# First neighbour aggregation between masked sums and attention heads, input stage at the step's end, three rotating x buffers: a four-layer graph network on one Trainium2 core

## The chip, the cores and the metric

One core of one Trainium2 chip runs the whole program. The metric is the device time of one execution in microseconds (us). The core has five engines that run their own instruction streams and meet only at semaphores: TensorE (PE in the profile; PEld is its weight load), VectorE (DVE), ScalarE (ACT), GpSimd (POOL) and SyncE (SP), the last of which here only issues DMAs.

## What is computed

Eight graphs of N = 1024 nodes with D = 128 features and a 0/1 adjacency matrix of 1024 x 1024 each. Every layer adds its result to its input and normalises the rows:

```python
x = _layernorm(x + _L0_gnn_ref(x, adj, Wq, bq, Wk, Wv, bv))   # masked softmax attention, 1 head
x = _layernorm(x + _L1_gnn_ref(x, adj, W, b))                 # mean over neighbours, linear, leaky ReLU
x = _layernorm(x + _L2_gnn_ref(x, adj, W, a))                 # 4 additive (GAT) heads of 32 features
x = _layernorm(x + _L3_gnn_ref(x, adj, B))                    # normalised adjacency (+ identity), linear
```

In the third layer `e = s_i + s_j`, with a leaky ReLU of slope 0.2, a softmax over the neighbours `i` of each `j`, and the weighted sum of `Wh`. Since exp(leaky(s_i + s_j)) is one product of exponentials where s_i + s_j is positive and another where it is negative, the kernel computes, for each head, sums over the neighbours above the step (matrices `c`, one per head, built from `steps` and `adj`) and sums over all neighbours (`mask` sums), and combines them.

## The kernel before

The rows of a graph lie in T = 8 tiles of 128 on the partitions. The work is pipelined over nine steps: "first" (graph 0 alone), seven "full" steps 1 to 7, and "last". Full step g does layers 0 and 1 of graph g, and layers 2 and 3 of graph g - 1 (called `o` in the code); "last" does layers 2 and 3 of graph 7. The order on every engine is written out by hand; engines are in order, so a wait holds everything behind it on its engine.

TensorE writes into four PSUM buffers of 128 x 1024 float32: three of a `ring`, claimed in turn by the groups of a fixed sequence (`claim` waits until the group three places earlier has been read), and `Z` for what is accumulated over a long time. In a full step TensorE does, in this order:

- **opening**: `xT` (transpose of the new x0), `q`, `v`; `s` 0 to 4 (bfloat16 scores, from which VectorE takes row maxima); between them, for the older graph, `x2T`, `wh` twice and `sj`, the inputs of its heads. At L1138 are `s`, at L1152 and L1165 `wh` and `sj`.
- **softmax**: eight transposed score groups `st` (L1198 adds the mask, L1200 the float32 scores), with `s` 5 to 7 between them, and one group later the `context` (L1222), which multiplies the exponentials that ScalarE made of the group. Two small transposes (`turn_largest` L1178, `spread_largest` L1183) are put between them.
- **heads**: `mask` 0 and 1 (L1235), then `c` 0 to 3 (L1254), one per head.
- **aggregations**: `agg1` (L1271, layer 1 of graph g: 32 matmuls), `out1` (L1287, times W1), `agg3` (L1271, layer 3 of the older graph) with the second half of `out1` inside, and `out3` (L1287) in two halves.

VectorE, for each row tile of the new graph, takes the row maximum of scores and mask (L755), rounds it (L742) and subtracts it from the mask (L747): together `guards`. A transposed score group needs the four mask tiles of its half. VectorE also builds `c` by a minimum of `steps` and `adj` (`mins`, L810), 32 tiles in a full step; evaluates each head (`combine`, L893 to L909); does layer 1's end (`layer1_out`, L927 to L932) and layer 3's (`layer3_out`, L940); the statistics of each norm (L839), its application (L846), and the splits of x into two float32r parts (`split_x1`, `split_x3`: L853, L855, L869).

ScalarE reads the ring (L579, L624), makes `maskb` for the coming graph (L591), the exponentials (`exp_tile`, L661), the `steps` tiles (L654; the list PACE says how many behind each exponential; four buffers, so tile n waits for the minimum of tile n - 4), and widens adjacency tiles from float16 to float32r for the aggregations (L612). These wide tiles have eight buffers: four of `wide_low`, and four of `wide_high`, which lie over `maskb`.

GpSimd computes each norm's rstd (L468, L471), the degrees (L455 to L461), the products of `wh` and `ex` (L497), two of the four subtractions that split them into three bfloat16 parts (L506 twice per piece), adds the identity to the transposed adjacency of the older graph (L526), applies the third norm (L480, L483), and issues the loads of `adj`. SyncE's queue transposes adjacency tiles by DMA: `adjT` for the new graph, and for the older one into `cmat[:, 1]`, which is possible only when head 1 has been computed (`turn_older`: `full["c"]`, 4).

x lives in four buffers: x0 (input), x1, x2 and x3 (after the first, second and third layer). In "last" the row of head 0 is made on TensorE (L1159), not fetched from DRAM.

## Time and profile before

| | |
|---|---|
| time, median of 3 runs | 977.44 us (975.45 to 979.87) |
| the profiled execution | 977.33 us, its span 975.5 us |
| mean granted TensorE clock | 0.957 |
| PE busy | 848.5 us, 87% of the span |
| DVE busy | 731.0 us, 75% |
| ACT busy | 587.1 us, 60% |
| POOL busy | 326.3 us, 33% |
| TensorE in step 5 (528.5 to 642.6 us) | busy 103.76 us of 114.10 |

The profile divides the span by instructions. A number in brackets at the end of a line of its timeline is the idle time of that engine just before, with what ended it. Several instructions of the same kind in a row are one line of the timeline, with their count; the time on it reaches from the first one's start to the last one's end, and includes waits of less than a fraction of a microsecond. Ends of matmuls are modelled, and 0.15 to 0.2 us of each lie beside the next one.

### The profile page before, as it was taken

The numbers are of one execution on the slowest core, as the hardware profiler recorded it, in microseconds if no ns is written. First come the engines' busy times: TensorE is split into PE (matmuls) and PEld (weight loads), VectorE is DVE, ScalarE is ACT, GpSimd is POOL, SyncE is SP. The second block draws the span as 40 slices with busy tenths as digits, with TensorE's granted clock in tenths as the row PEclk, the third lists the DMA queues.
The fourth block names the chain that finished last, engine by engine and source line by source line (L and its number), as shares of the span: only waits on it lengthen the run. The fifth ranks groups of instructions, "written<-read, shape, count | busy, mean of one in ns | idle before, by whom it ended". The sixth has DMA issues, their size and how long they took to land.

```text
span 975.5 us, 25298 instructions
## 1 busy us (share of the span) xinstructions
PE 848.5 (87%) x10856; PEld 683.6 (70%) x10856; DVE 731.0 (75%) x1635; ACT 587.1 (60%) x668; POOL 326.3 (33%) x335
## 2 busy tenths in 40 slices
PE   4988999798998989889998989989899899974874
PEld 2664699556985679746896569856697468962873
DVE  3438777788768787689777887687877798765965
ACT  1564675667665766656846666657665667545513
POOL 2022511633034520626007240355207161064404
PEclk8998999999999999999999999999999999996897
DMA  9823116911178123760268211781237601700260
GB/s 184 123 65 70 41 46 89 164 54 44 50 105 153 45 87 53 121 134 2 87 90 151 66 44 46 97 164 46 76 59 130 111 20 67 89 2 23 67 89 22
DMA packets 166463, 77.39 MB, mean 79 GB/s; under 512 B 136624, under 2 KB 154160, under 8 KB 166352
## 3 DMA queue, kind: packets, MB, share of 16 engines
q1 hardware_dynamic: 156864, 58.48, 31.5%
q0 software_dynamic: 8448, 16.78, 9.7%
q8 instruction: 85, 1.39, 0.6%
q10 hardware_dynamic: 1040, 0.52, 0.2%
q14 instruction: 26, 0.21, 0.1%
HBM read 54.66 MB, written 4.33 MB: 60 GB/s over the span
## 4 chain that ended last, share of the span: by engine, by line
PE 36%; issue 25%; DVE 22%; POOL 7%; ACT 7%; DVEq 0%; POOLq 0%; ACTq 0%
PE ring L1200 7%; PE Z L1222 7%; PE ring L1254 5%; PE Z L1271 4%; DVE x L846 4%; DVE cmat L810 4%; DVE ring L755 3%; PE ring L1235 2%; ACT steps L654 2%; POOL rstd L471 2%; ACT maskb L591 2%; PE ring L1198 2%; DVE meanvar L839 2%; PE ring L1165 1%; DVE x L830 1%
## 5 line engine op out<-in xcount | busy, mean ns | idle before, releaser
L654 ACT ACTIVATE steps<-sjrow,steepsi 128x1024 bf16<-128x1024 f32 x248 | 267.5, 1139 | 123.3 <-DVE cmat L810 94.9
L810 DVE TENSOR_TENSOR cmat<-steps,adj 128x1024 f16<-128x1024 bf16 x180 | 153.6, 896 | 24.6 <-ACT steps L654 22.6
L1254 PE MATMUL ring<-vparts,cmat 128*128 128x66 bf16 x4416 | 146.2, 195 | 16.9 <-DVE cmat L810 12.1
L1222 PEld LDWEIGHTS Z<-vv,probs 128*128 128x128 f32 x1024 | 122.6, 191 | 52.6 <-ACT probs L661 37.3
L1254 PEld LDWEIGHTS ring<-vparts,cmat 128*128 128x128 f16 x4416 | 143.5, 98 | 18.4 <-issue 7.4
L1222 PE MATMUL Z<-vv,probs 128*128 128x129 f32 x1024 | 126.5, 277 | 25.4 <-ACT probs L661 25.4
L1200 PE MATMUL ring<-qT,xT 128*128 128x512 f32 x256 | 139.4, 627 | 0.0
L526 POOL TENSOR_TENSOR cmat<-cmat,ident 128x1024 f16<-128x1024 f16 x8 | 17.1, 2144 | 254.1 <-DMA cmat<-adj 254.1
L755 DVE CUSTOM_DVE_ANT_0 ring<-ring,maskb 128x1024 f32<-128x1024 f32 x64 | 78.3, 1227 | 29.0 <-PE ring L1138 16.3
L661 ACT ACTIVATE probs<-ring 128x1024 f32<-128x1024 f32 x64 | 65.0, 1015 | 52.1 <-PE ring L1200 52.1
L1235 PE MATMUL ring<-vparts,adj 128*128 128x132 bf16 x1536 | 94.0, 222 | 0.0
L1235 PEld LDWEIGHTS ring<-vparts,adj 128*128 128x128 f16 x1536 | 93.3, 96 | 0.1
L1271 PE MATMUL Z<-wide_low,parts 128*128 128x512 f32 x256 | 68.7, 416 | 22.1 <-DVE parts L855 18.6
L846 DVE TENSOR_SCALAR x<-x,meanvar,rstd 128x128 f32<-128x128 f32 x192 | 73.7, 450 | 4.4 <-POOL rstd L471 4.4
L468 POOL TENSOR_SCALAR vareps<-meanvar 128x4 f32<-128x4 f32 x64 | 13.4, 210 | 186.5 <-DVE meanvar L839 185.5
L1271 PEld LDWEIGHTS Z<-wide_low,parts 128*128 128x128 f32 x256 | 48.0, 197 | 36.2 <-DVE parts L855 21.3
L471 POOL TENSOR_TENSOR rstd<-vareps,powers 128x4 f32<-128x4 f32 x64 | 71.1, 1111 | 5.4
L1198 PEld LDWEIGHTS ring<-ident,maskb 128*128 128x128 f16 x512 | 39.1, 99 | 43.8 <-issue 41.2
L1271 PE MATMUL Z<-wide_high,parts 128*128 128x512 f32 x256 | 65.6, 398 | 0.6 <-ACT wide_high L612 0.6
L612 ACT ACTIVATE wide_high<-adjT 128x1024 fp32r<-128x1024 f16 x32 | 31.2, 1048 | 45.5 <-PE ring L1254 45.5
L591 ACT ACTIVATE maskb<-adj 128x1024 f16<-128x1024 f16 x56 | 58.2, 1042 | 0.0
L1271 PEld LDWEIGHTS Z<-wide_high,parts 128*128 128x128 f32 x256 | 46.4, 188 | 10.8 <-ACT wide_high L612 2.4
(126 smaller groups left out, 1376.3 us busy)
## 6 DMA issues: line engine op xcount, KB each, us to landing
adj<-in_adj_dram POOLq DMA_DIRECT2D x16, 1024.0 KB, 13.0
sjrow<-sj_rows SPq DMA_DIRECT2D x31, 512.0 KB, 4.1
out_dram<-x SPq DMA_DIRECT2D x16, 256.0 KB, 2.4
x<-in_x_dram SPq DMA_DIRECT2D x7, 512.0 KB, 4.3
adjT<-adj SPq DMA_TRANSPOSE x64, 3.5
cmat<-adj SPq DMA_TRANSPOSE x64, 4.5
...
```

Of the source, the lines that this page charges most:

```text
L471: pool.tensor_tensor(rstd[:, layer, ts], vareps[:, layer, ts], powers[:, 0:4, 0], ALU.pow)\
L591: act.activation(maskb[:, t, :], adjs[g.parity][:, t, :], ACT.Copy, bias=-NEG, scale=NEG, accum_out=rowacc[g.parity][:, t:t + 1]).then_inc ...
L654: act.activation(steps[:, n % STEPS, :], sjrow[:, h % 2, :], ACT.Relu, bias=steepsi[:, t, h:h + 1], scale=STEEP).then_inc(step_made, 1)
L661: act.activation(probs[:, n % 2, :, :], slot(kind, "st", n)[:, :, :], ACT.Exp).then_inc(read["st"], 1)
L755: dve.tensor_tensor_reduce(out=s, in0=s, in1=maskb[:, t, :], scale=1.0, scalar=LOWEST, op0=ALU.add, op1=ALU.max, accum_out=smax[:, t:t + 1 ...
L810: dve.tensor_tensor(c_of[:, t, :], steps[:, n % STEPS, :], adjs[o.parity][:, t, :], ALU.min)\
L846: ins = dve.tensor_scalar(xn[:, t, :], xn[:, t, :], meanvar[:, layer, t, 1:2], rstd[:, layer, t:t + 1], ALU.subtract, ALU.mult)
L1200: last = pe.matmul(s[:, j, :], xT[:, kt * P:(kt + 1) * P], qT[:, c * 512:(c + 1) * 512], start=False, stop=True, skip_group_check=True)
L1222: last = pe.matmul(zq[:, q, 0:D + 1], probs[:, n % 2, j, q * P:(q + 1) * P], vv[:, kt, :], start=kt == 0 and q % 2 == 0, stop=kt == T - 1, ...
L1235: last = pe.matmul(s[:, j, 0:H * HW], adjs[o.parity][:, t, jt * P:(jt + 1) * P], vparts[:, t, :, part, HW:VW], start=t == 0 and part == 0, ...
L1254: last = pe.matmul(s[:, jt, 0:VW], c_of[:, t, jt * P:(jt + 1) * P], vparts[:, t, h, part, :], start=t == 0 and part == 0, stop=t == T - 1 ...
L1271: last = pe.matmul(Z[:, c, :], parts[:, part, t, :], wide(t)[:, c * 512:(c + 1) * 512], start=t == 0 and part == 0, stop=t == T - 1 and pa ...
```

## The change

The order on TensorE in a full step becomes: `s` 1 to 4, the softmax, `mask` 0 and 1, `agg1`, `c` 0, `out1` twice, `c` 1 to 3, then for graph g `x2T`, `wh`, `wh`, `sj` and mixed with them for graph g + 1 `xT`, `q`, `v`; then `agg3`, `out3` with `s` 0 of graph g + 1 between its halves. One list SEQ over all steps gives each group its place in the ring. The wide tiles are reduced from eight to four buffers (the second four are widened only when TensorE has used the first four), and `adjT` takes both the transposed adjacency of the new graph and, when that has been widened, of the older one. Three buffers rotate for x, each worked on in place through the four layers. VectorE and ScalarE get the same reordering. The subtraction of the values' high part moves from GpSimd to VectorE. PACE becomes two tiles behind every exponential but the first. "last" fetches all four rows from DRAM.

```diff
+    def groups_of(n):
+        def of(graph, *names):
+            return [(name, graph, k) for name, k in names] if 0 <= graph < NB else []
+        seq = []
+        if n == 0:
+            seq += of(0, ("xT", 0), ("q", 0), ("v", 0))
+        if n < 2:
+            seq += of(n, ("s", 0))
+        seq += of(n, *[("s", t) for t in range(1, 5)])
+        for t in range(T):
+            seq += of(n, ("st", t))
+            if t < 3:
+                seq += of(n, ("s", 5 + t))
+        masks, c = [("mask", 0), ("mask", 1)], [("c", h) for h in range(H)]
+        if n < NB:
+            seq += of(n - 1, *masks, c[0])
+        else:
+            seq += of(n - 1, c[0], *masks)
+        seq += of(n, ("out1", 0), ("out1", 1))
+        seq += of(n - 1, *c[1:])
+        if n < NB:
+            seq += of(n, ("x2T", 0)) + of(n + 1, ("xT", 0)) + of(n, ("wh", 0), ("wh", 1)) + of(n + 1, ("q", 0)) \
+                + of(n, ("sj", 0)) + of(n + 1, ("v", 0))
+        seq += of(n - 1, ("out3", 0))
+        if n > 0:
+            seq += of(n + 1, ("s", 0))
+        return seq + of(n - 1, ("out3", 1))
+    SEQ = [group for n in range(NB + 1) for group in groups_of(n)]
+    PLACE = {group: n for n, group in enumerate(SEQ)}
+    assert len(PLACE) == len(SEQ)
...
-    PACE = [0, 2, 2, 3, 3, 2, 2, 3]
+    PACE = [0, 2, 2, 2, 2, 2, 2, 2]
...
-        wide_low = sb("wide_low", [P, T // 2, N], F32R)
+        wide = sb("wide", [P, T // 2, N], F32R)
...
-        wide_high = sharing("wide_high", [P, T // 2, N], F32R)
         cmat = sb("cmat", [P, 2, T, N], F16)
-        adjT_of_older = cmat[:, 1, :, :]
...
-        x1 = sb("x1", [P, T, D], F32)
-        x2 = sb("x2", [P, T, D], F32)
-        x3 = sb("x3", [P, T, D], F32)
+        xs = [sb(f"x_{n}", [P, T, D], F32) for n in range(3)]
+        def x_of(g):
+            return xs[g.base % 3]
...
-        def wide(t):
-            return wide_low[:, t, :] if t < T // 2 else wide_high[:, t - T // 2, :]
-        def uses_until(agg, g, t):
+        def wide_used_by(agg, g, t):
             n = max(0, 2 * g.base - 1) if agg == "agg1" else min(2 * g.base + 2, 2 * NB - 1)
-            return (T - 1) * (n - 1) + t + 1
+            return (T - 1) * n + t - 3 if t >= T // 2 else (T - 1) * (n - 1) + t + 5
...
-                if g.base > 0:
-                    sp.wait_ge(widened["agg1"], g.count(T))
+                if g.base == 1:
+                    sp.wait_ge(widened["agg1"], T)
+                elif g.base > 1:
+                    sp.wait_ge(widened["agg3"], g.before(2).count(T, T))
...
+            def turn_older(kind, o):
+                if kind == "last":
+                    sp.wait_ge(widened["agg3"], o.count(T))
+                else:
+                    sp.wait_ge(widened["agg1"], o.count(T, 2 * T))
...
+                if kind != "last":
+                    if g.base < NB - 1:
+                        sp.wait_ge(y_made[0], g.count(2, 2))
+                        sp.dma_start(x0[:, :, :], x_v[number(Graph(g.base + 1))]).then_inc(x_in, 16)
+                    if kind == "full":
+                        turn_older(kind, o)
+                    spread_sj(g)
+                    for h in (0, 1):
+                        fetch_sj(kind, g, h)
...
-                    if 1 + SPLIT_BY_DVE[kind] <= n < pieces + 1:
-                        take_off(kind, o, n - 1, 0, None, high_made, rest_made)
                     if n >= 2 + SPLIT_BY_DVE[kind]:
-                        take_off(kind, o, n - 2, 1, 2, middle_made, low_made)
+                        low_part(kind, o, n - 2)
...
                 if kind != "last":
                     rstd_of(0, g)
+                    degree_of(g)
+                    for k in range(2):
+                        rstd_of(1, g, [k])
                 if kind != "first":
                     add_diagonal(o)
-                    rstd_of(2, o)
                     if o.base < NB - 2:
                         pool.wait_ge(full["mask"], o.count(2, 2))
                         pool.wait_ge(c_made, o.count(H * T, H * T))
                         load_adj(Graph(o.base + 2))
-                if kind != "last":
-                    degree_of(g)
-                if kind != "first":
+                    rstd_of(2, o)
...
-                    act.activation(wide(t), src, ACT.Copy).then_inc(widened[agg], 1)
+                    if t >= T // 2 or (t < T // 2 - 1 and (agg == "agg3" or g.base > 0)):
+                        act.wait_ge(wide_used, wide_used_by(agg, g, t))
+                    act.activation(wide[:, t % (T // 2), :], adjT[:, t, :], ACT.Copy).then_inc(widened[agg], 1)
...
-                    widen(kind, g, "agg1", range(T))
+                            made = steps_until(made + PACE[n])
+                    widen(g, "agg1", range(0, 4))
+                    if kind == "first":
+                        make_maskb(Graph(1), range(4, T))
+                    else:
+                        made = steps_until(20)
+                    widen(g, "agg1", range(4, T))
                     take_sums("agg1", g, agg1T)
...
+                if kind != "first":
+                    made = steps_until(len(STEP_TILES[kind]))
+                    widen(o, "agg3", range(0, 4))
+                if kind != "last":
+                    following = Graph(g.base + 1)
+                    for name, graph, k in (("x2T", g, 0), ("xT", following, 0), ("wh", g, 0), ("wh", g, 1),
+                                           ("q", following, 0), ("sj", g, 0), ("v", following, 0)):
+                        if graph.base < NB:
+                            take_group(kind, graph if name != "sj" else g, name, k)
+                if kind != "first":
+                    widen(o, "agg3", range(4, T))
+                    take_sums("agg3", o, agg3T)
...
+                if part == 0:
+                    v = VALS[kind][:, :, hs, :]
+                    dve.wait_ge(high_made, o.count(NP, n + 1 - SPLIT_BY_DVE[kind]))
+                    dve.tensor_tensor(v, v, vparts[:, :, hs, 0, :], ALU.subtract).then_inc(rest_made, 1)
...
+                    mins(kind, o, 1, range(0, 4))
+                norm_apply(0, g, x_of(g), 0)
                 split_x1(g, 0)
...
                 if kind == "full":
+                    mins(kind, o, 1, range(4, T))
                     sums_of_masks(kind, o, 0)
-                    mins(kind, o, 2)
-                    sums_of_masks(kind, o, 1)
-                norm_apply(0, g, x1, 1)
+                norm_apply(0, g, x_of(g), 1)
                 split_x1(g, 1)
                 if kind == "full":
+                    mins(kind, o, 2, range(0, 4))
+                    sums_of_masks(kind, o, 1)
+                    mins(kind, o, 2, range(4, T))
                     combine(kind, o, 0)
-                    mins(kind, o, 3)
-                    last_heads(kind, o)
                 for k in range(2):
                     layer1_out(kind, g, k)
-                    norm_stats(1, g, x2, k)
-                final = g.base == NB - 1
-                if kind == "full" and not final:
...
+                if kind == "full":
+                    mins(kind, o, 3, range(0, 4))
+                    combine(kind, o, 1)
+                    mins(kind, o, 3, range(4, T))
+                norm_apply(1, g, x_of(g), 0)
+                norm_apply(1, g, x_of(g), 1)
+                if kind == "full":
+                    combine(kind, o, 2)
+                    end_of_heads(kind, o)
+                    split_x3(o, 0)
+                    split_x3(o, 1)
+                largest_si(g)
+                if g.base < NB - 1:
+                    cast_x(Graph(g.base + 1))
+                    cast_q(Graph(g.base + 1))
+                if kind == "full":
                     layer3_out(kind, o, 0)
...
-                early = [(c, t) for c in range(2) for t in range(T // 2)]
+            def aggregate(of, agg, parts, second_half):
+                early = [(c, t) for t in range(T // 2) for c in range(2)]
                 late = [(c, t) for c in range(2) for t in range(T // 2, T)]
...
                     for n in range(T):
                         scores(kind, g, n)
                         if kind == "full" and n == 0:
-                            turn_largest(kind, g.before())
-                        if between_scores[n]:
-                            group(kind, g, *between_scores[n])
-                        if kind == "full" and n == 0:
-                            spread_largest(kind, g.before())
+                            turn_largest(kind, o)
+                        if n < 3:
+                            guard_scores(kind, g, 5 + n)
+                        if kind == "full" and n == 1:
+                            spread_largest(kind, o)
                         if n >= 1:
                             context(kind, g, n - 1)
```

Three places of the order. The first is TensorE's heads and aggregations in the full steps 2 to 6 (`parts1` marks agg1, `parts3` agg3, `w1_s` out1, `b3_s` out3; `vparts,adj0` are the mask sums, the others with `vparts` the heads 0 to 3). Before:

```order
L1235 MATMUL ring0<-vparts,adj0 128x132 x96
L1254 MATMUL ring1<-vparts,cmat 128x66 x192
L1254 MATMUL ring2<-vparts,cmat 128x66 x192
L1254 MATMUL ring0<-vparts,maskb 128x66 x192
L1254 MATMUL ring1<-vparts,cmat 128x66 x192
L1271 MATMUL Z<-wide_low,parts1 128x512 x16
L1271 MATMUL Z<-wide_high,parts1 128x512 x14
L1287 MATMUL ring2<-w1_s,qT 128x128 x4
```

The same place of the change:

```order
L1249 MATMUL ring0<-vparts,adj0 128x132 x96
L1283 MATMUL Z<-wide,parts1 128x512 x32
L1268 MATMUL ring1<-vparts,cmat 128x66 x192
L1297 MATMUL ring2<-w1_s,qT 128x128 x4
L1297 MATMUL ring0<-w1_s,qT 128x128 x4
L1268 MATMUL ring1<-vparts,cmat 128x66 x192
L1268 MATMUL ring2<-vparts,maskb 128x66 x192
L1268 MATMUL ring0<-vparts,cmat 128x66 x192
```

The aggregation of the new graph and head 0 stand ahead of out1, and the heads 1 to 3 behind it.

The second place is TensorE between out3 and the first transposed scores. Before (`qxb` are the `s` groups, `identf` the two transposes, `wext` wh and sj):

```order
L1287 MATMUL ring2<-b3_s,x2T 128x128 x4
L1109 MATMUL ring0<-identf,x0 128x128 x8
L1122 MATMUL ring1<-xT,wqk 128x512 x2
L1129 MATMUL ring2<-wv_s,xT 128x128 x8
L1138 MATMUL ring0<-qxb 128x512 x2
L1109 MATMUL ring1<-identf,x2 128x128 x8
L1138 MATMUL ring2<-qxb 128x512 x2
L1138 MATMUL ring0<-qxb 128x512 x2
L1152 MATMUL ring1<-wext,x2T 128x136 x4
L1138 MATMUL ring2<-qxb 128x512 x2
L1152 MATMUL ring0<-wext,x2T 128x136 x4
L1165 MATMUL ring1<-x2T,wext 4x512 x2
```

The same place of the change:

```order
L1162 MATMUL ring0<-qxb 128x512 x2
L1297 MATMUL ring1<-b3_s,x2T 128x128 x4
L1162 MATMUL ring2<-qxb 128x512 x2
L1162 MATMUL ring0<-qxb 128x512 x2
L1162 MATMUL ring1<-qxb 128x512 x2
L1162 MATMUL ring2<-qxb 128x512 x2
L1212 MATMUL ring0<-ident16,maskb 128x128 x4
```

Of the projections, transposes and head inputs none stands between the `s` groups any more; they are ahead of agg3.

The third place is VectorE behind head 0 (`small` and `ring` with `probs` begin a `combine`, L945 to L950 are layer1_out, L826 the mins of head 3). The change:

```order
L924 TENSOR_TENSOR x<-small,x 128x8x32
L945 SCALAR_TENSOR_TENSOR rest<-ring,rrow,b_s 128x128 x4
L948 SCALAR_TENSOR_TENSOR rest<-rest 128x512
L950 TENSOR_TENSOR x<-x,rest 128x512
L855 BN_STATS meanvar<-x 128x6 x2
L945 SCALAR_TENSOR_TENSOR rest<-ring,rrow,b_s 128x128 x4
L948 SCALAR_TENSOR_TENSOR rest<-rest 128x512
L950 TENSOR_TENSOR x<-x,rest 128x512
L855 BN_STATS meanvar<-x 128x6 x2
L826 TENSOR_TENSOR cmat<-steps,adj 128x1024 x4
L909 TENSOR_TENSOR small<-probs,ring 128x264
```

Before, the minima of head 3 followed `combine` 0 directly, all eight in a row; now layer1_out with its statistics stands ahead of them, and `combine` 1 between their halves.

## Rows read from the trace of the kernel before

**Rows 1.** Busy time by stretch: step 5 and "last" (us; sum, then engines with counts).
```profile
528.50:642.60 114.10, 103.76 (x1358) 83.84 (x1356) 89.59 (x202) 73.96 (x85) 39.41 (x41) 0.99 0.44 84
874.20:975.50 101.30, 62.08 (x1046) 55.01 (x1044) 71.17 (x151) 39.53 (x40) 36.07 (x36) 0.79 0.25 48
```
**Rows 2.** Waits of TensorE: total us, times, longest.
```profile
PE Z L1222 <- ACT probs L661: 25.4, 19, 1.7
PE Z L1271 <- DVE parts L855: 18.6, 7, 10.7
PE ring L1122 <- ACT xT L579: 16.9, 6, 3.1
```
**Rows 3.** Timeline of TensorE: first transposed scores of steps 1, 2, 5, 7.
```profile
91.78 0.39 PE L1198 MATMUL ring<-ident,maskb 128*128 128x128 f16 x4
...
202.70 0.39 PE L1198 MATMUL ring<-ident,maskb 128*128 128x128 f16 x4
...
545.83 0.39 PE L1198 MATMUL ring<-ident,maskb 128*128 128x128 f16 x4
...
774.53 0.39 PE L1198 MATMUL ring<-ident,maskb 128*128 128x128 f16 x4
```
**Rows 4.** Timeline of TensorE, end of step 4, opening of step 5.
```profile
526.04 0.71 PE L1271 MATMUL Z<-wide_high,parts 128*128 128x512 f32 x2
527.53 1.13 PE L1287 MATMUL ring<-b_s,x2T 128*128 128x128 f32 x8 [0.78 <-ACT x2T L597]
528.50 1.04 PE L1109 MATMUL ring<-identf,x 128*128 128x128 f32 x8
532.59 2.68 PE L1122 MATMUL ring<-xT,wqk 128*128 128x512 f32 x4 [3.05 <-DVE x L940]
```
**Rows 5.** Timeline of VectorE, the same stretch.
```profile
526.98 1.11 DVE L927 SCALAR_TENSOR_TENSOR x<-ring,rrow,b_s 128x128 f32<-128x128 f32 x4
...
530.32 2.14 DVE L940 SCALAR_TENSOR_TENSOR x<-ring,dcol,x 128x128 f32<-128x128 f32 x8
...
538.59 1.23 DVE L755 CUSTOM_DVE_ANT_0 ring<-ring,maskb 128x1024 f32<-128x1024 f32 x1 [1.34 <-PE ring L1138]
...
544.40 0.87 DVE L747 TENSOR_SCALAR maskb<-maskb,guard 128x1024 f16<-128x1024 f16 x2
```
**Rows 6.** Timeline of TensorE: last context, mask sums, a head, end of step 5.
```profile
584.16 2.05 PE L1222 MATMUL Z<-vv,probs 128*128 128x129 f32 x16 [0.93 <-ACT probs L661]
586.05 11.76 PE L1235 MATMUL ring<-vparts,adj 128*128 128x132 bf16 x192
597.65 12.10 PE L1254 MATMUL ring<-vparts,cmat 128*128 128x66 bf16 x384
...
640.11 0.71 PE L1271 MATMUL Z<-wide_high,parts 128*128 128x512 f32 x2
```
**Rows 7.** Timeline of VectorE: minima beside GpSimd, the minimum of tile 7, combine, minima.
```profile
570.27 3.75 DVE L810 TENSOR_TENSOR cmat<-steps,adj 128x1024 f16<-128x1024 bf16 x3
...
578.36 3.09 DVE L810 TENSOR_TENSOR cmat<-steps,adj 128x1024 f16<-128x1024 bf16 x5
...
603.95 0.43 DVE L893 TENSOR_TENSOR small<-probs,ring 128x264 f32<-128x264 f32 x1 [2.73 <-PE ring L1254]
...
606.60 3.69 DVE L810 TENSOR_TENSOR cmat<-steps,adj 128x1024 f16<-128x1024 bf16 x6
```
**Rows 8.** Timeline of GpSimd: a subtraction beside the first of them.
```profile
570.44 2.43 POOL L506 TENSOR_TENSOR vparts<-cmat,vparts 128x1056 bf16<-128x1056 f32 x1 [2.65 <-DVE vparts L793]
```
**Rows 9.** Timeline of "last": VectorE, GpSimd and TensorE ahead of agg3.
```profile
947.01 0.76 DVE L839 BATCH_NORM_STATS2 meanvar<-x 128x6 f32<-128x256 f32 x2
...
948.66 2.11 POOL L526 TENSOR_TENSOR cmat<-cmat,ident 128x1024 f16<-128x1024 f16 x1 [27.82 <-DMA cmat<-adj]
...
955.58 6.14 PE L1271 MATMUL Z<-wide_low,parts 128*128 128x512 f32 x16 [10.67 <-DVE parts L855]
```
**Rows 10.** Timeline of TensorE: end of step 0.
```profile
72.23 1.13 PE L1287 MATMUL ring<-w_s,qT 128*128 128x128 f32 x8 [0.78 <-ACT qT L597]
```

424 lines of the change are left out of this document (183 added, 241 removed).

## The prediction

> **What bounds the kernel now.** I read first the busy time by stretch: in a full step TensorE is busy 103.8 of 114.1 us, in "last" 62.1 of 101.3 [rows 1]. So TensorE bounds the middle, where some 10.3 us of a step are idle, and chains of waits bound both ends. Then the waits of TensorE: three groups make up half of its idle time [rows 2], namely contexts that wait for exponentials (25.4 us), aggregations for the split parts (18.6, of which 10.7 once) and `q` for xT read (16.9, some 3 us a step). Then I took one mark per step, the first transposed score group [rows 3]. Steps 2 to 7 follow each other at (774.53 - 202.70) / 5 = 114.4 us; step 1 takes 110.9; the first mark stands at 91.8; behind the last lie 975.5 - 774.5 = 201.0.
>
> The change does not lessen TensorE's work: the same matmuls, less one group of two in "last". It can only move waits. I therefore lay out a full step in three pieces, from rows of steps 4 and 5, and then both ends. "Mark" is always that first score group.
>
> **Piece 1: from the first half of out3 to the mark.** Before, 526.04 to 545.83: 19.8 us [rows 3, 4], in which stand `xT`, `q`, `v`, `s`, `x2T`, `wh`, `sj`, and the waits 0.78 and 3.05 [rows 4]. Now these projections and head inputs come ahead of agg3: x2T and xT about 1 each (as xT in rows 4), the two wh 2.1, q 2.5, sj 1.8, v 2.75 and 0.4 for x2T to be read: 11.5 us. Between them each reading by ScalarE is covered by the next group, so the 3.05 goes. But behind out3's first half only 3.6 us of work remain: the end of agg3, out3's second half and five `s` groups of 0.44. And VectorE's chain does not get shorter. It has to wait for out3's second half, which is done 2.5 us on; 0.2 for the semaphore and 1.1 for that half of layer3_out (2.14 for both [rows 5]) make 3.8. Then come the guards of tiles 0 to 3, from 538.59 to 545.2, 6.6 us [rows 5], and these have to be complete before the mark. So the mark stands 10.4 us behind, with some 6.7 us idle: guards that were hidden by wh, sj and x2T are bare. Piece 1 becomes 11.5 + 10.4 = 21.9: **+2.1 us**. Here the 3 us won at `q` are given back, and more.
>
> **Piece 2: softmax, from the mark to the mask sums.** Before, 545.83 to 586.05: 40.2 us [rows 3, 6]. The last contexts waited because ScalarE's exponential 6 stood behind a `steps` tile that needed the minimum of tile 7, done about 579.0 [rows 7], and exponential 7 behind two or three more. With PACE at two, only exponential 7 stands behind it. VectorE gets to tile 7 at the same place: behind the mark by 33 to 34 us. Two added subtractions of 1.3 us each (128 x 1056 float32; estimate from 0.69 for 512 columns) fit ahead of context 0, where VectorE waited 2 us; the later place of `spread_largest` costs 1 us more of guards and some 0.7 of the first context, in place of TensorE's wait of 0.8. Step tile 33.8 to 34.9, exponential to 35.9, last context 1.8: mask sums start at 37.9. **-2.3 us**. Bounds: -4.7, if no context waits, and 0, if the subtractions are met by GpSimd's and push tile 7 out.
>
> **Piece 3: mask sums to out3's first half.** Before, 586.05 to 640.11: 54.1 us [rows 6]. Gone is agg3's wait for its parts, 18.6 - 10.7 over six steps: -1.3, since 11.5 us of openings and two splits' margin of about 4 us stand ahead. Four wide tiles in place of eight: a widening and the matmuls on its tile take about 1 us each, with the first four ready: +0.1. agg1 follows the mask sums (11.7 us); its parts need VectorE's context 1, norm and split, about 9.8 us: hidden, the second half by the first. What is new is head 3. Its first accumulation needs all eight minima. From head 0's end VectorE has: 0.3 to start; combine 2.65 (603.95 to 606.60 [rows 7]); layer1_out with statistics, twice 3.34 (526.98 to 530.32 [rows 5]); four minima at 0.62 (3.69 for six [rows 7]); combine 1, 2.65; four minima more, 2.5: together 17.3. TensorE has out1 1.6, two heads of 6.0 (12.1 for two [rows 6]) and 0.65 of head 3 until it asks for tile 7: 14.2. The wait is 3.1, and longer where GpSimd's diagonal addition of 2.1 us [rows 9] falls in: it now comes behind the second rstd of layer 1, so right there. I take +3.5. Piece 3: **+2.3 us**.
>
> What VectorE does next is late with it, but hidden: norm 1 is done 2.2 us behind the last minimum, head 3 takes 5.3, so x2T does not wait; combine 2 and 3, statistics and the splits take until some 7 us behind head 3's end, ahead of agg3, which comes 11.5 behind it. DMA: the transposes of the older adjacency start when agg1 has been widened, 17 us behind the mask sums' start, and take some 16 with their landing; head 3 is over at 48. `adj`, x0 and the rows of s_j are asked for no later than before, relative to their use.
>
> The sum of a step: 2.1 - 2.3 + 2.3 = +2.1, times five: **+10.5**. Step 1 had few waits to lose (no older graph to finish): +1.8 - 0.8 + 2.9 = **+3.9**.
>
> A shared resource decides how far the 3.5 goes up. Three minima took 3.75 beside GpSimd's subtraction of 2.43 us, where three alone take 1.9 [rows 7, 8]: 1.9 us lost for 2.4 of overlap. By that, 2.1 us of diagonal addition cost up to 1.6. The Trainium skill (SBUF — State Buffer, "Who interferes with whom") says that a VectorE instruction with two SBUF inputs and a GpSimd one that reads SBUF exclude each other for a whole instruction. By that, head 3's wait would be anything from 3.1 to 5.2, by who comes first; the sum would lie between -3 and +12 us of mine. These rows agree with it roughly.
>
> **The start.** In step 0 nothing hides the new order. `x2T` needs norm 1 of graph 0, and before, xT, q and v of graph 1 stood in front of it. agg1 with four wide tiles costs 2 more, since four `maskb` tiles stand between them on ScalarE. out1, whose second half began at 72.2 [rows 10], ends at 75; layer1_out twice 3.34 from 74.4, rstd 1.4 and half a norm 1.1 give x2T at 83.8; 12.3 of openings, 0.6 of `s`, 6.6 of guards: mark at 103.4, against 91.8 [rows 3]. **+11.6 us**.
>
> **The end.** Three things. Head inputs of graph 7 and the row of s_j lie before agg3 of graph 6, where VectorE catches up: some 4 to 5 us fewer between the two graphs' heads, after +2 for head 3's wait. The transposes and the diagonal addition, which ended at 950.8 [rows 9], are done long before the heads; then agg3 waits only for statistics (947.77 [rows 9]) and one split of 2.25, so stands at 950.0 and not 955.58: -5.6. Step 7's softmax gives its 2.3. The sum is **-12 us** (189 for 201). Bounds: -6, and -16 if TensorE's clock, which was 0.79 there [rows 1], recovers.
>
> **Sum.** 11.6 + 3.9 + 10.5 - 12 = +14 us on the profiled execution's 977.33, whose span is 975.5, and 0.1 below the median: 991 us.
>
> **The rivals.**
> - *VectorE is in time for head 3* (ends on the other side). If VectorE gained over 3 us between head 0 and tile 7 (or c3 asked later), the wait of 3.5 would be none in seven steps: 991 - 24.5 = 966. For it: all its parts are short instructions that may overlap more than their starts show. Against: the 17.3 are measured start to start; the point of decision is 14.2. Chance 0.12.
> - *The exponentials no longer hold contexts.* Piece 2 at its bound: 2.4 us more in six steps, 991 - 14 = 977: no change. For: PACE gives exponential 6 three microseconds of room. Against: tile 7's place on VectorE. Chance 0.18.
> - *VectorE and GpSimd exclude each other* wherever they were moved together (diagonal addition beside minima, split beside norm 2): 2 us more a step, 1004. Chance 0.15.
>
> **How the numbers follow.** The forecast, slower by 0.7 to 2.2%, has 0.55. The time 991 is that of this case alone. Its own range is 984 to 999; down to 974 for the second rival and half way to the first, up to 1005 for the third. About 0.5% (5 us) is what a measurement here can tell from no change: faster 0.12, the same 0.18, slower 0.70.
>
> **What would show it.** TensorE's waits: `q` for xT gone; about 5 to 7 us a step for VectorE's maxima and guarded `maskb`, at `s` 2, `s` 4 and the mark; a new wait of 3 to 4 for `cmat` in head 3; none for parts in the middle, some 5 us in "last". The first mark near 103, steps of 116.5, 189 behind the last. I would be wrong in the main term if the steps were 114 or shorter: then either `cmat` shows no wait, or the guards end sooner than 10 us behind out3's first half. I would be wrong on piece 2 if contexts still wait 4 us a step.

## The result and the profile after

The changed kernel takes 1004.7 us (median) against 977.1 for the kernel before in the same rounds: ratio 1.0275, 95% interval 1.0244 to 1.0306. Three of its four runs lie between 1003.4 and 1004.8; the fourth took 1238.9 us at a mean granted clock of 0.657 and is left out of the ratio. The change makes the kernel slower, by 27.6 us. The forecast said slower with 0.70 and 991 us, 13.7 too low. 1004.7 lies above the forecast's own range of 984 to 999, and 0.3 below the 1005 that it allowed for its third rival.

The profiled execution took 1003.4 us with a span of 1001.6. The head of its page: busy time by engine, then the granted TensorE clock in 40 slices.

```profile
PE 861.8 (86%) x10852; PEld 690.3 (69%) x10852; DVE 746.3 (75%) x1652; ACT 588.4 (59%) x667; POOL 297.1 (30%) x318
...
PEclk9997899979999999998999999997999999998788
```

TensorE does no more work than before but is busy 13.3 us longer: its mean granted clock is 0.937, before 0.957. The marks (first transposed score group of steps 1, 2, 5 and 7), which answer to [rows 3]:

```profile
102.44 0.59 PE L1212 MATMUL ring<-ident,maskb 128*128 128x128 f16 x4 [3.57 <-DVE maskb L759]
...
218.61 0.59 PE L1212 MATMUL ring<-ident,maskb 128*128 128x128 f16 x4 [3.13 <-DVE maskb L759]
...
572.31 0.44 PE L1212 MATMUL ring<-ident,maskb 128*128 128x128 f16 x4 [3.57 <-DVE maskb L759]
...
807.91 0.53 PE L1212 MATMUL ring<-ident,maskb 128*128 128x128 f16 x4 [3.57 <-DVE maskb L759]
```

None of them waited before; and four small matmuls that took 0.39 us there take up to 0.59.

| part (us of the profiled execution) | before | predicted | after |
|---|---|---|---|
| start to first mark | 91.8 | 103.4 | 102.4 |
| step 1 | 110.9 | 114.8 | 116.2 |
| a step, mean of five | 114.4 | 116.5 | 117.9 |
| behind the last mark | 201.0 | 189 | 193.7 |

Where TensorE waits (total us, times, longest), the rows that answer to [rows 2]:

```profile
PE ring L1268 <- DVE cmat L826: 27.4, 32, 2.4
PE ring L1212 <- DVE maskb L759: 27.3, 8, 3.6
PE ring L1162 <- DVE smax L767: 14.0, 10, 2.0
PE Z L1236 <- ACT probs L664: 9.0, 6, 1.5
```

The waits of `q` for xT are gone, the parts are waited for once (5.1 us, in "last"), contexts wait 9.0 us and not 25.4. In their place come the minima of head 3 (`cmat`), the guarded `maskb` at the mark, and row maxima (`smax`). The stretch around the mark of step 5 on TensorE shows the last two, and what follows them:

```profile
563.40 1.13 PE L1297 MATMUL ring<-b_s,x2T 128*128 128x128 f32 x8 [0.33 <-ACT x2T L611]
564.37 0.59 PE L1162 MATMUL ring<-qxb 128*128 128x512 bf16 x2
566.95 1.79 PE L1162 MATMUL ring<-qxb 128*128 128x512 bf16 x6 [1.99 <-DVE smax L767]
572.31 0.44 PE L1212 MATMUL ring<-ident,maskb 128*128 128x128 f16 x4 [3.57 <-DVE maskb L759]
572.54 2.02 PE L1214 MATMUL ring<-qT,xT 128*128 128x512 f32 x2
574.36 0.63 PE L1212 MATMUL ring<-ident,maskb 128*128 128x128 f16 x4
574.78 1.64 PE L1214 MATMUL ring<-qT,xT 128*128 128x512 f32 x2
```

The matmuls behind out3's first half start at 561.91 and the mark stands 10.4 us on, as worked out. But two score matmuls that take 1.08 us elsewhere take 2.02 and 1.64 here. The busy time by stretch says why (columns as in [rows 1]: stretch, length, PE, PEld, DVE, ACT, POOL, then granted clock):

```profile
562.00:572.31 10.31, 4.28 (x23) 1.85 (x21) 8.87 (x25) 8.90 (x17) 0.00 (x0) 1.00 1.00 172
572.31:577.33 5.02, 5.02 (x20) 2.22 (x21) 1.97 (x5) 0.87 (x1) 0.00 (x0) 0.66 0.02 3
```

TensorE is busy 4.3 of the 10.3 us ahead of the mark, and in the five us behind it the granted clock is 0.66: for part of them it is at 1.2 instead of 2.4 GHz. The loss is a third of 5 us, 1.7 us. This is the milder of two cases that take turns. In steps 2, 4 and 6 the clock is at 1.2 GHz from some 4.5 us ahead of the mark to some 6 us behind it (step 6, around the mark at 689.64); why the two cases take turns was not taken apart:

```profile
685.00:689.64 4.64, 1.41 (x5) 0.17 (x4) 4.64 (x15) 3.89 (x8) 0.00 (x0) 0.51 0.79 149
689.64:694.66 5.02, 5.02 (x14) 1.93 (x14) 1.69 (x4) 0.35 (x1) 0.00 (x0) 0.50 0.02 5
```

From the mark to the mask sums it takes 38.8 us in steps 3, 5 and 7 and 39.8 to 39.9 in steps 2, 4 and 6. A second loss lies in head 3, behind its wait for minima:

```profile
640.00:679.00 39.00, 35.07 (x613) 30.08 (x610) 34.71 (x79) 18.80 (x20) 17.49 (x18) 0.96 0.49 98
```

That is 0.04 of 39 us, 1.6. The kernel before had a loss of this size too, but only one a step: ahead of its mark, where `q` and `v` run behind the wait of `q`, and none behind the mark.

```profile
526.00:536.00 10.00, 6.17 (x30) 4.05 (x29) 9.73 (x28) 6.34 (x11) 5.82 (x6) 0.88 1.11 201
536.00:545.83 9.83, 9.25 (x52) 5.67 (x52) 8.21 (x22) 4.06 (x6) 0.00 (x0) 0.94 0.32 60
545.83:550.80 4.97, 4.17 (x24) 2.02 (x23) 2.59 (x10) 4.97 (x10) 0.00 (x0) 1.00 0.36 91
```

1.2 + 0.6 = 1.8 us a step before. Over the five steps the whole cost shows in TensorE's busy time, for the same matmuls before and after:

```profile
202.70:774.53 571.83, 519.56 (x6781) 419.40 (x6780) 452.74 (x1010) 369.64 (x421) 199.98 (x200) 0.99 0.44 84
218.61:807.91 589.30, 530.81 (x6780) 425.52 (x6781) 464.23 (x1021) 371.32 (x420) 184.42 (x190) 0.96 0.42 82
```

TensorE is busy 11.3 us longer, 2.25 us a step, and stands idle 1.2 us a step longer: of the 3.5 us that a step grows, two thirds are slower matmuls and one third is waiting.

### The profile page after: what moved, and what is told of

The parts are those of the page before. It is cut to its first block, busy times and chain, and to the rows that moved or that the text cites. A ratio compares the mean times of both kernels' runs of the same rounds, so it can differ in the third digit from the quotient of the medians.

```text
span 1001.6 us, 25308 instructions
## 1 busy us (share of the span) xinstructions
PE 861.8 (86%) x10852; PEld 690.3 (69%) x10852; DVE 746.3 (75%) x1652; ACT 588.4 (59%) x667; POOL 297.1 (30%) x318
## 4 chain that ended last, share of the span: by engine, by line
PE 53%; DVE 33%; issue 6%; ACT 5%; POOL 0%; DVEq 0%; POOLq 0%; ACTq 0%
PE ring L1268 12%; PE Z L1283 11%; PE ring L1249 9%; DVE cmat L826 7%; PE ring L1214 6%; DVE ring L767 4%; PE Z L1236 4%; DVE x L862 3%; DVE meanvar L855 2%; ACT maskb L605 2%; DVE rest L945 2%; PE ring L1212 2%; PE ring L1177 2%; DVE vparts L805 2%; DVE cmat L810 2%
## 5 line engine op out<-in xcount | busy, mean ns | idle before, releaser
L1268 PE MATMUL ring<-vparts,cmat 128*128 128x66 bf16 x4416 | 161.9, 200 | 43.0 <-DVE cmat L826 27.4
L1268 PEld LDWEIGHTS ring<-vparts,cmat 128*128 128x128 f16 x4416 | 155.5, 102 | 49.7 <-DVE cmat L826 31.5
L1214 PE MATMUL ring<-qT,xT 128*128 128x512 f32 x256 | 151.8, 677 | 0.0
L621 ACT ACTIVATE wide<-adjT 128x1024 fp32r<-128x1024 f16 x128 | 124.7, 1045 | 38.1 <-PE Z L1283 38.1
L826 DVE TENSOR_TENSOR cmat<-steps,adj 128x1024 f16<-128x1024 bf16 x180 | 136.3, 806 | 13.0 <-ACT steps L657 11.0
L1283 PE MATMUL Z<-wide,parts 128*128 128x512 f32 x512 | 128.4, 403 | 9.7 <-DVE parts L871 5.1
L1283 PEld LDWEIGHTS Z<-wide,parts 128*128 128x128 f32 x512 | 94.0, 190 | 35.4 <-ACT wide L621 9.6
L826 DVE TENSOR_TENSOR maskb<-steps,adj 128x1024 f16<-128x1024 bf16 x62 | 40.6, 688 | 66.3 <-ACT steps L657 66.3
L1212 PE MATMUL ring<-ident,maskb 128*128 128x128 f16 x512 | 53.0, 230 | 27.3 <-DVE maskb L759 27.3
L1162 PE MATMUL ring<-qxb 128*128 128x512 bf16 x128 | 40.1, 409 | 17.0 <-DVE smax L767 14.0
```

Source lines behind the costliest of these rows:

```text
L621: act.activation(wide[:, t % (T // 2), :], adjT[:, t, :], ACT.Copy).then_inc(widened[agg], 1)
L826: dve.tensor_tensor(c_of[:, t, :], steps[:, n % STEPS, :], adjs[o.parity][:, t, :], ALU.min)\
L1212: pe.matmul(s[:, j, q * P:(q + 1) * P], maskb[:, 4 * c + q, kt * P:(kt + 1) * P], ident16[:, :], start=q == 0, stop=False, skip_group_chec ...
L1214: last = pe.matmul(s[:, j, :], xT[:, kt * P:(kt + 1) * P], qT[:, c * 512:(c + 1) * 512], start=False, stop=True, skip_group_check=True)
L1268: last = pe.matmul(s[:, jt, 0:VW], c_of[:, t, jt * P:(jt + 1) * P], vparts[:, t, h, part, :], start=t == 0 and part == 0, stop=t == T - 1 ...
L1283: last = pe.matmul(Z[:, c, :], parts[:, part, t, :], wide[:, t % (T // 2), c * 512:(c + 1) * 512], start=t == 0 and part == 0, stop=t == T ...
```

## The experiments

The theory after reading the result: (A) the idle time costs twice, once as itself and once by the clock behind it; the rest is what the prediction says. Its rivals: the placing of the heads' inputs (B), the minima of head 3 (C), or the subtraction on VectorE (D) cost more than I took. Each kernel is the changed one with the main part of its edit shown (`...` marks what is left out), unless said otherwise. Each was timed in turn with the kernel before on its chip: 978.9 us beside x1, x2, x3 and x5, 980.4 beside x4, x6, x7 and x8, 979.7 beside x9 and x10, 978.9 beside x11 and x12.

**x1_filler.** In steps 2 to 7, 22 matmuls a step whose result nobody reads, in the two waits ahead of the mark; a step's own work and its order stay.

```diff
+            def idle_work(count):
+                for _ in range(count):
+                    pe.matmul(Z[:, 0, :], qb[:, 0:P], xb[:, 0:512], start=True, stop=True)
...
                     for t in range(1, 5):
                         guard_scores(kind, g, t)
+                        if g.base > 1 and t == 1:
+                            idle_work(7)
+                    if g.base > 1:
+                        idle_work(15)
```

> The changed kernel, and in steps 2 to 7 TensorE gets 22 more bfloat16 matmuls of 512 columns between the s groups and the first transposed scores (7 behind s 1, 15 behind s 4), into Z, read by nobody, some 4.8 us in the place of 5.6 us of waiting. Theory A (the wait at the mark lets the granted clock fall, and the scores behind it pay): the first two score groups come back from about 4.2 us to 2.3 each pair of them, steps get shorter by 1 to 2 us although TensorE has more to do, 1004.7 becomes 993 to 999. Rival (the clock is lower for another reason, or the scores are slow for their mask): no step gets shorter, 1004 to 1008.

Measured: 995.5 us, ratio 1.0162 (1.0139 to 1.0186), 9 us less than the changed kernel with more work on TensorE. A step takes 116.07 us, 1.8 less. The stretch behind the mark of step 5 in this kernel:

```profile
558.40:568.81 10.41, 9.13 (x46) 4.11 (x45) 8.86 (x25) 8.90 (x17) 0.00 (x0) 1.00 0.97 173
568.81:573.80 4.99, 4.99 (x28) 2.40 (x29) 1.97 (x5) 1.02 (x1) 0.00 (x0) 1.00 0.00 0
```

The guards are ready as late as before (10.4 us), and no clock is lost, here or behind the mark of any other step with fillers. From the mark to the mask sums it takes 37.1 us in every one of them, not 38.8 and 39.8. The score matmuls (L1214) fall from 677 to 633 ns on the mean; times 256 that is 11 us of TensorE's time. The added matmuls do nothing that the kernel needs, and the guards come no sooner, so what is gained is gained by the clock: (A) is shown, about 9 us.

**x2_mins3.** All minima of head 3 ahead of combine 1.

```diff
-                    mins(kind, o, 3, range(0, 4))
+                    mins(kind, o, 3)
                     combine(kind, o, 1)
-                    mins(kind, o, 3, range(4, T))
```

> The changed kernel with one edit on VectorE: all eight minima of head 3 ahead of combine 1, not four ahead and four behind. Theory A (head 3 waits for VectorE's chain): the 3.4 us of TensorE's waits for cmat in head 3 fall by the 2.65 to 4 us of combine 1, to less than 1 us; seven steps give 19 to 24 us, so 981 to 986. Rival B (what VectorE is late with moves on: norm 1, combine 2 and 3 and the splits now end as late as before, and agg3 takes over the wait): agg3 waits 2 to 3 us for its parts in each step and the gain is 5 us or less, 999 to 1004.

Measured: 1006.1 us, ratio 1.0268 (1.0250 to 1.0286): nothing gained. TensorE's waits tell where it went:

```profile
PE ring L1176 <- DVE small L911: 20.0, 7, 3.1
PE ring L1267 <- DVE cmat L826: 13.9, 32, 1.7
```

The wait for minima is halved, but a new one of 3.1 us stands in each of seven steps, where the first `wh` claims its slot. Neither text named this place. The group three places ahead of it in SEQ is head 3, so the slot is free when combine 3 has read it:

```profile
665.15 0.29 DVE L911 TENSOR_TENSOR small<-ring,ex 128x132 f32<-128x132 f32 x1
```
```profile
665.50 2.12 PE L1176 MATMUL ring<-wext,x2T 128*128 128x136 f32 x16 [3.06 <-DVE small L911]
```

Combine 3 comes behind all eight minima, combine 1, the norm and combine 2 in either order, so VectorE is done with it no sooner. The edit only lets TensorE arrive earlier. This is the rival's reason (what VectorE is late with moves on), one place ahead of where the rival looked for it.

**x3_heads.** `x2T`, `wh` twice and `sj` of the older graph back between the `s` groups, behind agg3, on all engines; `xT`, `q`, `v`, and everything else, as in the change.

```diff
...
+                    if kind == "full":
+                        head_inputs(o, "x2T", 0)
                     for t in range(1, 5):
                         guard_scores(kind, g, t)
+                        if kind == "full" and t == 2:
+                            head_inputs(o, "wh", 0)
+                        if kind == "full" and t == 3:
+                            head_inputs(o, "wh", 1)
+                            head_inputs(o, "sj", 0)
...
```

> The changed kernel, with x2T, wh and sj of the older graph put back between the s groups 0 to 4 behind agg3, and only xT, q and v of the next graph ahead of it; the first aggregation, the buffers and the subtraction stay as changed. Theory A (the guards are bare): the waits for row maxima and guarded masks fall from about 5.6 us a step to below 2, the clock behind the mark stays up, x2T of graph 0 no longer holds the first step; against it xT is read bare again, 1.3 us. Steps of 112 to 114 us, the first mark near 93, in all 968 to 980. Rival (agg3 needs the whole opening as cover): it waits 2 us or more for its parts, steps of 116, 990 or more.

Measured: 978.5 us, ratio 0.9989 (0.9974 to 1.0004): no different from the kernel before, 26 us less than the changed one. Steps are 114.4 long and the first mark is at 96.2. The head inputs cost nothing where they fill the waits for guards, and there they also keep the clock (1.00 in the five us behind the marks of steps 2 to 7). The wait for `cmat` is still 26.6 us. So (B) is the largest part; it holds most of (A), since of the 3.5 us that a step gets shorter, 1.9 lie between the mark and the mask sums (37.6 us against 39.4 on the mean).

**x5_poolsub.** The values' high part is subtracted on GpSimd again.

```diff
+            def take_off_high(kind, o, n):
...
+                pool.tensor_tensor(v, v, vparts[:, :, hs, 0, :], ALU.subtract).then_inc(rest_made, 1)
...
-                if part == 0:
-                    v = VALS[kind][:, :, hs, :]
-                    dve.wait_ge(high_made, o.count(NP, n + 1 - SPLIT_BY_DVE[kind]))
-                    dve.tensor_tensor(v, v, vparts[:, :, hs, 0, :], ALU.subtract).then_inc(rest_made, 1)
```

> The changed kernel with the subtraction of the values' high part on GpSimd again. Theory A: it was hidden by VectorE's wait for context 0, and its return to GpSimd slows the minima beside it: same within 3 us, 1002 to 1008. Rival (the added 2.5 us of VectorE in each step is what made the change slow): 985 to 995.

Measured: 1006.0 us, ratio 1.0266 (1.0247 to 1.0286), no different from the change. (D) falls: the place of this subtraction is worth nothing here.

**x7_before_pace.** The kernel before with one line changed.

```diff
-    PACE = [0, 2, 2, 3, 3, 2, 2, 3]
+    PACE = [0, 2, 2, 2, 2, 2, 2, 2]
```

> The kernel before with the pace of two steps for every tile instead of three for some, nothing else: piece 2 of the prediction alone. If the threes held the exponentials and these the contexts, TensorE's wait for probs falls from 25.4 us in sum to under 12, and the whole takes 964 to 971. Rival: what the contexts no longer wait is waited for the minima that then get their steps later (mask sums or head 0 wait longer), and the time stays within 974 to 980.

Measured: 959.5 us, ratio 0.9788 (0.9753 to 0.9823). Its first three groups of waits:

```profile
PE Z L1271 <- DVE parts L855: 22.1, 8, 10.3
PE ring L1122 <- ACT xT L579: 19.5, 7, 3.1
PE ring L1254 <- DVE cmat L810: 12.1, 6, 7.1
...
PE Z L1222 <- ACT probs L661: 9.0, 6, 1.5
```

A step takes 112.0 us and not 114.4: -2.4. From the mark to the mask sums it is 37.25 and not 40.2, -3.0, where piece 2 said -2.3; 0.6 comes back in the rest of the step. I had set the whole gain too low: with step 1 (2.2) and what lies behind the last mark (3.3) it is 18 us. The waits for probs fall by 16.4 us, to 9.0, and no other wait grows by more than 3.5.

**x12_after_threes.** The reverse in the changed kernel.

```diff
-    PACE = [0, 2, 2, 2, 2, 2, 2, 2]
+    PACE = [0, 2, 2, 3, 3, 2, 2, 3]
```

> The changed kernel with the old pace (three steps for some tiles), nothing else: what the pace alone is worth inside the change. In the kernel before, the twos alone gave 18 to 21 us (x7_before_pace). Theory: piece 2 is the same in both kernels, so this is 15 to 21 us slower than the changed kernel: 1020 to 1026, with 25 us of waits for probs. Rival: with the order of the change the threes would have cost less, since its contexts start behind a wait that already gives ScalarE a lead: 1005 to 1014.

Measured: 1024.2 us, ratio 1.0460 (1.0431 to 1.0489), waits for probs 25.4 us again. The two edits add up: the pace is worth 18 to 21 us in either order, and all the rest of the change costs some 45 (959.5 to 1004.7, or 978.9 to 1024.2).

**x4_ends.** In the last step the sums of masks behind the minima; in the first `xT`, `q`, `v` of graph 1 ahead of graph 0's head inputs.

```diff
+                mins(kind, o, 2)
                 sums_of_masks(kind, o, 0)
-                mins(kind, o, 2)
...
+                if kind == "first":
+                    for name in ("xT", "q", "v"):
+                        project(kind, following, name)
+                    for name, k in (("x2T", 0), ("wh", 0), ("wh", 1), ("sj", 0)):
+                        head_inputs(g, name, k)
```

> The changed kernel with its two ends reordered and the five steps between left alone: at the start x is transposed and q and v are made ahead of the heads' matmuls of graph 0, and in the last step VectorE takes the sums of masks behind head 2's minima. If the two misses of the ends are what I read them to be (sums of masks ahead of minima hold combine 0 and so head 1's claim at the end; at the start the second graph's cast waits on work it does not need), head 1's wait for small in the last step falls from 5.1 to about 2 us, the first mark of step 1 comes at 93 to 98 instead of 102.4, and the whole takes 990 to 997. Rival: the start's 8 us are only moved, because the heads' row-copies then come late for step 1's minima, and the mark of step 2 stands where it stood: 998 to 1003. A step in the middle stays at 117.3 to 118.2 by both.

Measured: 1000.9 us, ratio 1.0213 (1.0179 to 1.0248). The end gives 2.3 us (191.4 behind the last mark) and the wait for `small` falls to 3.7; the first mark does not come sooner at all: 103.6, where the change has 102.4. All seven groups stand ahead of `s` 1 in either order, and the guards bound the mark. x3_heads, where four of them stand behind, has it at 96.2. My theory of the start was wrong.

**x8_heads_last** and **x6_best**: on to a faster kernel, from x3_heads. The first moves `xT` ahead of head 3, where TensorE waits for minima, and takes over the last step of x4_ends; the second adds two moves on VectorE, and one on ScalarE that the text ahead of the run does not name: between the two halves of agg3 that it reads, ScalarE makes the first `maskb` tile.

```diff
                     for h in range(1, H):
+                        if h == 3 and following.base < NB:
+                            project(kind, following, "xT")
                         head_sums(kind, g, h)
```

```diff
+                late_norm = kind == "full" and g.base < NB - 1
...
+                if late_norm:
+                    norm_apply(1, g, x_of(g), 0)
+                    norm_apply(1, g, x_of(g), 1)
...
                     layer3_out(kind, o, 0)
+                    if g.base < NB - 1:
+                        row_maximum(kind, Graph(g.base + 1), 0)
                     layer3_out(kind, o, 1)
...
-                    take_sums("agg3", o, agg3T)
+                    take_sums("agg3", o, agg3T, [0])
                 if kind == "full" and g.base < NB - 1:
-                    make_maskb(Graph(g.base + 1), range(0, 4))
+                    make_maskb(Graph(g.base + 1), [0])
+                if kind != "first":
+                    take_sums("agg3", o, agg3T, [1])
+                if kind == "full" and g.base < NB - 1:
+                    make_maskb(Graph(g.base + 1), range(1, 4))
```

> x3_heads (heads' matmuls of the older graph spread between the score guards, 978.5 us) with two more moves: the transposes of the following x stand ahead of head sum 3, where TensorE waits 2.4 + 3 x 0.33 us for head 3's minima, and in the last step the sums of masks stand behind the minima. Theory: the transposes fill the wait, but what they give up is waited for VectorE's split ahead of aggregation 3 (its first half was ready when TensorE came, its second 0.66 us late), so only about 1 us a step is gained: 965 to 975. Rival: the wait for the minima was no shorter than the transposes and nothing else is late: 2 to 3 us a step, 957 to 965.

> x8_heads_last with two moves on VectorE: the normalisation of layer 1 stands behind the split of x3 instead of ahead of it (2.3 us earlier split; x2 is transposed only behind aggregation 3 here), and the row maximum of the first score tile stands between the two halves of layer 3's result, so that the guard of the following graph comes some 1.2 us sooner. If the split is what holds x8, this takes 4 to 10 us off it: 957 to 968. Rival: the waits at the split were covered already, and both are equal within 2 us.

Measured: 973.4 us, ratio 0.9938 (0.9915 to 0.9962), and 963.8 us, ratio 0.9833 (0.9795 to 0.9872); the profiled execution of x6_best is its slowest, 967.8 us. In x8_heads_last a step is as long as in x3_heads (114.3); the waits for `cmat` fall from 26.6 to 22.0 and those for `parts` rise from 7.3 to 19.8. So what the transposes fill is waited for at the split. In x6_best a step is 113.0, but not for the reason that I gave: the wait at the split is the same, 1.6 us, with the norm ahead of it or behind it. What went is the wait for the row maximum of `s` 0. In x8_heads_last TensorE stands still there for 1.54 us:

```profile
660.07 1.04 PE L1180 MATMUL ring<-qxb 128*128 128x512 bf16 x4 [1.54 <-DVE smax L783]
```

In x6_best another has come for it, for the casts ahead of `s` 0, which now stand behind the norm:

```profile
653.73 0.59 PE L1191 MATMUL ring<-qxb 128*128 128x512 bf16 x2 [1.27 <-DVE qxb L1033]
```

Of the 1.3 us that a step is shorter, 0.5 are less idle time on TensorE and 0.8 are less busy time for the same matmuls (519.8 us and not 523.8 in five steps). Which of the three moves gives them was not taken apart.

**x9_casts**: the casts of x and q ahead of the norm, half of the norm earlier. **x10_casts_mins3** adds x2_mins3. **x11_bias_late** adds to x9_casts one wait on GpSimd.

```diff
-                norm_apply(1, g, x_of(g), 0)
-                norm_apply(1, g, x_of(g), 1)
+                if kind == "first":
+                    cast_x(Graph(1))
+                    cast_q(Graph(1))
                 if kind == "full":
                     combine(kind, o, 2)
+                norm_apply(1, g, x_of(g), 0)
+                if g.base == NB - 1:
+                    norm_apply(1, g, x_of(g), 1)
+                if kind == "full":
                     end_of_heads(kind, o)
...
```

```diff
             def bias_x0(g):
+                if g.base > 1:
+                    pool.wait_ge(full["s"], g.count(PER["s"], 1))
                 pool.wait_ge(full["xT"], g.count(1, 1))
```

> x6_best with VectorE's order changed once more: the casts of the following x and q stand ahead of the normalisation of layer 1 in the first step (there TensorE waits 5.95 us for them), and in the steps between only the second half of that normalisation is left behind the split and behind the casts, its first half filling a 1.3 us gap ahead of head 3's result. Theory: VectorE's row from the split to the fourth row maximum, which runs without a gap in x6_best, is what TensorE waits for there (1.55 + 0.85 + 1.27 us a step); it becomes some 2.5 us shorter, so the first mark of step 1 comes 4 to 6 us sooner and a step takes 111 to 112.3 instead of 113.0: 945 to 956. Rival: the split itself is bound by head 3's sums on TensorE and the guards by ScalarE's guard tiles, so only the start gains: 957 to 961.

> x9_casts with all minima of head 3 ahead of combine 1, as in x2_mins3. There the wait only moved, to a claim of head 1's slot of the ring; here head sum 3 itself claims that slot. Theory: combine 1 has read the slot about 1 us behind the last minimum, so TensorE starts head sum 3 some 1 us sooner and without the three pauses of 0.33 us, and gains 1 to 1.5 us a step on x9_casts: 5 to 10 us less. Rival: VectorE is the bound by then (its work up to head 3's result is the same), and the waits at the split take the gain: equal within 2 us.

> x9_casts with one wait more on GpSimd: the bias is added to the following x (2.84 us on GpSimd, at 643.5 to 646.3 in x9_casts) only when the first guard scores are made. While it ran, VectorE's two casts took 1.52 and 2.88 us; in the first step, without GpSimd beside them, and in x6_best each took 0.68. Theory: GpSimd's elementwise work is what makes VectorE's casts and scalings between SBUF tiles slow, so the casts fall to about 0.7 each (the first perhaps half) and VectorE's row to the fourth row maximum becomes 2 to 3 us shorter. TensorE waits for little of it, so the time falls by 0 to 6 us: 954 to 960. Rival: the casts are slow for another reason (they stay at 1.5 and 2.9), and the time stays.

Measured: 960.3 us (ratio 0.9810, 0.9781 to 0.9839), 964.0 (0.9832, 0.9793 to 0.9872) and 960.5 (0.9807, 0.9780 to 0.9839). The start gained 0.5 us: the casts are waited for 1.55 us there and not 5.95, but `x2T` now waits 3.4 us for the norm that stands behind them. A step gained 0.6 to 0.7. So the rival's number for x9_casts holds, though its place does not: the gain was in the steps. In x10_casts_mins3 the wait for minima falls from 21.9 to 5.2 us and the one for `small` grows from 3.5 to 18.1: head 3 claims the slot of head 1, which combine 1 has to read, and I had priced that claim too low. The rival, VectorE as the bound, fits better, but not by its place, the split; the time is 3.7 us above x9_casts, and the intervals overlap. In x11_bias_late the second cast fell as the theory said; the first stayed at 1.5 us, for it stands beside another GpSimd operation (1.37 us) that was not moved, and ends some 0.55 us behind it in both kernels. VectorE in x9_casts, GpSimd there, and VectorE in x11_bias_late:

```profile
642.54 1.52 DVE L1029 CAST qxb<-xT 128x1024 bf16<-128x1024 f32 x1
643.99 2.88 DVE L1033 CAST qxb<-qT 128x1024 bf16<-128x1024 f32 x1
```
```profile
642.15 1.37 POOL L516 TENSOR_TENSOR x<-x,rstd 128x512 f32<-128x512 f32 x1
643.48 2.84 POOL L479 TENSOR_TENSOR x<-x,bv_s 128x1024 f32<-128x1024 f32 x1
```
```profile
641.32 1.53 DVE L1031 CAST qxb<-xT 128x1024 bf16<-128x1024 f32 x1
642.77 0.68 DVE L1035 CAST qxb<-qT 128x1024 bf16<-128x1024 f32 x1
```

The second cast took 2.88 us beside GpSimd's bias and ended 0.55 behind it, and 0.68 with GpSimd idle. The time did not move: behind the casts and half a norm VectorE then waits 1.46 us for out3.

x7_before_pace and x9_casts are both about 2% faster than the kernel before (intervals 0.9753 to 0.9823 and 0.9781 to 0.9839) and the same as each other; x7_before_pace does it with one line. x7_before_pace has the shorter steps (112.0 us, and 197.7 behind the last mark), x6_best the shorter end (190.6); a kernel with both was not tried.

## Why the prediction came out as it did

**Direction and order of the parts: right.** Slower was forecast because guards would be bared and head 3 would wait for minima, and both stand in the trace. The mark is 10.4 us behind out3's first half (predicted 10.4). Head 3 waits 2.38 + 0.33 + 0.34 + 0.33 = 3.4 us a step (predicted 3.5):

```profile
652.94 0.27 PE L1268 MATMUL ring<-vparts,cmat 128*128 128x66 bf16 x3 [2.38 <-DVE cmat L826]
653.54 0.27 PE L1268 MATMUL ring<-vparts,cmat 128*128 128x66 bf16 x3 [0.33 <-DVE cmat L826]
654.15 0.27 PE L1268 MATMUL ring<-vparts,cmat 128*128 128x66 bf16 x3 [0.34 <-DVE cmat L826]
654.75 1.45 PE L1268 MATMUL ring<-vparts,cmat 128*128 128x66 bf16 x23 [0.33 <-DVE cmat L826]
```

That the figure is so close is in part luck: the sum left out 0.8 us of matmuls that TensorE does between these waits, and it took 0.4 for the diagonal addition, which costs 1.26 (see the rivals). x2_mins3 shows that the wait is not a cost by itself: with TensorE served earlier there, it waits for combine 3. It does not speak against the first rival (VectorE in time, 966 us), which needed VectorE's whole work to be shorter; what fails that rival is the wait itself.

**Pieces 1 and 3, all but the stretch behind the mark: right.** From the mask sums to the next mark it takes 78.5 us on the mean of the five steps (117.9 - 39.4); the forecast has 56.4 + 21.9 = 78.3, against 74.1 before. Two errors cancel in it. The openings take 9.9 us and not 11.5, because the rows that priced `q` and `v` come from the slow stretch of the kernel before; that loss, 1.7 us, now lies in head 3.

**The step that failed: the idle time of piece 1 was priced as idle time alone.** The text says "with some 6.7 us idle" (6.0 in the trace) and then sums piece 2, the matmuls behind it, at the clock of the kernel before. It is piece 2 that comes out too long, 39.4 us on the mean for the 37.9 worked out: 38.8 in the odd steps, where the clock is 0.66 in the five us behind the mark, and 39.8 to 39.9 in the even ones, where it is 0.50.

```profile
611.08 11.76 PE L1249 MATMUL ring<-vparts,adj 128*128 128x132 bf16 x192
...
729.43 11.76 PE L1249 MATMUL ring<-vparts,adj 128*128 128x132 bf16 x192
```

With the gap filled (x1_filler) piece 2 takes 37.1, better than worked out, as it is in x7_before_pace (37.25). So the clock costs 2.3 us a step behind the mark, and 0.8 of it is hidden in the number by a piece 2 that I had set too long. The steps are 1.4 us longer than worked out, 7 in five steps, and step 1 as much: 8.4 of the 12.1 us by which the span was too low (the start gives 1.0 back, the end takes 4.7). x1_filler, which fills only the gap ahead of the mark, gets 9 us back. The rows for it were there: in "last" TensorE was busy 62 of 101 us at 0.79 [rows 1], and I used that as a bound for a gain at the end, never for a loss in the steps.

**The start: right** (1 us less than worked out), and x3_heads shows its cause: 6 of the 11 us are the head inputs.

**The end: right in kind, 4.7 us short.** Agg3 of "last" waits 5.1 us and not 10.7 [rows 9], as said. What was left out: VectorE takes the sums of masks ahead of head 2's minima, so combine 0 is late and head 1 waits for its `small` 5.1 us, where the kernel before had 2.0. Moving them (x4_ends) gives 2.3 us back. The rest was not taken apart.

```profile
956.86 3.37 PE L1268 MATMUL ring<-vparts,cmat 128*128 128x66 bf16 x58 [5.09 <-DVE small L911]
```

**The rivals.** The second, exponentials that hold no context, did not come: contexts wait 9.0 us in all, 1.5 in each of six steps. The third predicted 1004 and the time is 1004.7; that they agree is luck. Its mechanism is in the trace, but the excess of the time is not: of the places that it named, head 3's wait is 3.4 us, my figure and not 2 more, and the split beside norm 2 is slowed (2.66 us, where its first half takes 1.10) but nothing waits for it. The diagonal addition does not meet the minima. It meets combine 1, one operation of which takes 1.68 us and not 0.42 in each of the seven steps; these 1.26 us are part of the 3.4:

```profile
648.01 2.35 POOL L543 TENSOR_TENSOR adjT<-adjT,ident 128x1024 f16<-128x1024 f16 x1
```
```profile
648.98 1.68 DVE L913 TENSOR_TENSOR small<-small,ex 128x264 f32<-128x264 f32 x1
```

That VectorE and GpSimd do exclude each other is shown by x9_casts and x11_bias_late; the Trainium skill (SBUF — State Buffer, "Who interferes with whom") says it of casts and scalings in their fast modes too, which my sentence on two inputs had left out, and the trace agrees: the cast that met the 2.84 us bias took 2.88 and not 0.68. In the changed kernel this does not explain what the forecast missed.
